# Two stacked fp32 attentions: the score products of the first, K = 16, placed on two 32-row tiles of TensorE

## The reference, cut to what matters

```python
# first block, per image (n = 256 pixels, d = 16)
f, g, hv = xf @ wf + bf, xf @ wg + bg, xf @ wh + bh
beta = softmax(einsum('bnd,bmd->bnm', g, f))
att  = gamma * (einsum('bnm,bmd->bnd', beta, hv) @ wo + bo) + xf
y    = relu(batchnorm(concatenate([att, xf], -1) @ wc + bc))
# second block: 8 heads of 16; keys and values from a 3x3 stride-2 average pool of y
out  = softmax(q @ k.T / 4) @ v          # 256 queries, 64 keys, per head
res  = (out @ w_o + b_o) + y
```

## Time and profile before

| what | us |
|---|---|
| median of 3 runs | 57.96 |
| lowest and highest of the 3 | 57.37, 60.24 |
| span of the profiled execution, first to last instruction | 58.4 |

### The profile page before, as it was taken

One profiled execution on the slowest core, in us unless ns is written; L12 is line 12 of the kernel. 1 busy time (PEld: TensorE's weight loads), 2 busy tenths in 40 slices (PEclk: granted clock), 3 DMA queues, 4 the chain that ended last, 5 costly groups with the idle time before them and its releaser, 6 DMA issues.

```text
span 58.4 us, 948 instructions
## 1 busy us (share of the span) xinstructions
PE 53.0 (91%) x314; PEld 41.1 (70%) x314; DVE 40.1 (69%) x114; ACT 30.5 (52%) x75; POOL 13.5 (23%) x25
## 2 busy tenths in 40 slices
PE   2998999999999999999999999999999999489630
PEld 2935584988786647899966899975889953459410
DVE  1005599300687819996979997998997989997920
ACT  4502333540766997999840899850785810443000
POOL 6779990000019000008300004700004000000000
PEclk9999999999999999999999999999999999999855
DMA  0798200000000000000000000000000200002211
GB/s 0 180 324 334 110 0 0 0 0 0 0 0 0 0 11 0 0 0 6 6 0 0 0 0 0 0 0 11 0 0 0 90 0 0 0 0 83 97 45 45
DMA packets 1300, 1.96 MB, mean 34 GB/s; under 512 B 144, under 2 KB 912, under 8 KB 1296
## 3 DMA queue, kind: packets, MB, share of 16 engines
q1 hardware_dynamic: 1296, 1.91, 9.9%
HBM read 1.38 MB, written 0.52 MB: 33 GB/s over the span
## 4 chain that ended last, share of the span: by engine, by line
PE 84%; DVE 9%; issue 1%; ACT 1%
PE bk_o L391 11%; PE bk_k L350 8%; PE bk_y L323 7%; PE bk_s1a L370 7%; PE bk_fg L266 5%; PE bk_s1b L370 4%; PE bk_s0a L300 4%; PE bk_y L319 4%; PE bk_s0b L300 4%; PE bk_s1b L376 4%; PE bk_k L416 4%; PE bk_fg L338 3%; PE bk_s0a L310 3%; DVE d L638 2%; PE bk_y L357 2%; PE bk_s1a L376 2%
## 5 line engine op out<-in xcount | busy, mean ns | idle before, releaser
L518 ACT ACTIVATE p<-d 128x512 f32<-128x512 f32 x8 | 5.0, 630 | 7.8 <-DVE d L638 7.7
L238 POOL TENSOR_TENSOR p0n<-p,rsum 128x256 f32<-128x256 f32 x6 | 3.5, 612 | 23.5 <-DVE rsum L594 23.5
L391 PE MATMUL bk_o<-v_heads,pt 128*128 128x34 f32 x56 | 6.9, 276 | 0.0
L391 PEld LDWEIGHTS bk_o<-v_heads,pt 128*128 128x128 f32 x56 | 6.6, 192 | 0.1
L350 PE MATMUL bk_k<-xp,late 128*80 128x64 f32 x64 | 5.3, 235 | 0.0
L584 DVE TENSOR_REDUCE nmax<-bk_s0a 128x1 f32<-128x256 f32 x4 | 1.7, 420 | 5.2 <-PE bk_s0a L300 5.2
L513 ACT COPY k_heads<-k_rows 32x128 f32<-32x128 f32 x16 | 4.7, 296 | 0.7
L350 PEld LDWEIGHTS bk_k<-xp,late 128*80 128x80 f32 x64 | 4.9, 151 | 0.3 <-DVE xp L603 0.2
L621 DVE COPY k_heads<-k_rows 32x128 f32<-32x128 f32 x16 | 4.4, 277 | 0.3
L323 PE MATMUL bk_y<-pt,val 128*128 128x256 f32 x16 | 4.6, 415 | 0.0
L370 PE MATMUL bk_s1a<-k_heads,q_heads 128*128 128x512 f32 x8 | 4.3, 615 | 0.1
(11 more groups left out here) (115 smaller groups left out, 113.5 us busy)
## 6 DMA issues: line engine op xcount, KB each, us to landing
late<-in_late SPq DMA_DIRECT2D x1, 522.5 KB, 5.7
x_rest<-in_x_rest SPq DMA_DIRECT2D x1, 384.0 KB, 4.9
out_t<-res SPq DMA_DIRECT2D x3, 128.0 KB, 1.8
prep<-in_prep SPq DMA_DIRECT2D x1, 291.5 KB, 2.8
first<-in_first SPq DMA_DIRECT2D x1, 153.5 KB, 2.4
out_t<-res SPq DMA_DIRECT2D x2, 64.0 KB, 1.6
```

Source lines behind the costliest of these rows:

```text
L238: nc.gpsimd.tensor_tensor(p0n[:, b, t, :], p0[:, b, t, :], rsum0[:, b, t:t + 1].to_broadcast([P, N]), ALU.mult).then_inc(p0_pool, 1)
L391: last = mm(o_ps[b][s][:, k * 2 * VW:(k + 1) * 2 * VW], pt1[:, b, s, k, :], v_heads[:, b, s * 2 + k % 2].rearrange("m h v -> m (h v)"), st ...
L518: sc.activation(p1[:, b, s, :], d1[:, b, s].rearrange("n h m -> n (h m)"), ACT.Exp, scale=1.0 / TEMP).then_inc(exp1_done, 1)
```

## The change

`wfg` becomes 128 columns wide: f, zeros, f, zeros, g, zeros, g, zeros, each copy of 16 columns at a multiple of 32. One product per image now fills all 128 PSUM partitions. The copies to `f` and `g` take 64 partitions each instead of 16, so that both tensors hold the values at partitions 0 to 15 and again at 32 to 47, with zeros (from the zero columns and zero biases) between. The score product of half `t` contracts over the 32 partitions from 32t instead of over 128: half 0 on rows 0 to 31 of TensorE, half 1 on rows 32 to 63. The two halves already wrote to two PSUM banks. The two memsets and the waits on them go. The DMA `first` grows by 80 columns of 128 rows.

```diff
-FIRST = {"wfg": 48, "bf": 1, "bg": 1, "var": 1, "x0": N}
+FIRST = {"wfg": P, "bf": 1, "bg": 1, "var": 1, "x0": N}
...
-            nc.gpsimd.memset(f[:], 0.0).then_inc(fg_clear, 1)
-            nc.gpsimd.memset(g[:], 0.0).then_inc(fg_clear, 1)
...
-                mm(fg_bank[b][0:48, 0:N], f_("wfg"), image(b), start=True, stop=True).then_inc(fg_ps, 1)
+                mm(fg_bank[b][:, 0:N], f_("wfg"), image(b), start=True, stop=True).then_inc(fg_ps, 1)
...
             def scores_0(b, t):
                 if t == 0:
-                    if b == 0:
-                        pe.wait_ge(fg_clear, 2)
...
-                mm(bk_s0[t][:, 0:N], g[:, b, t * P:(t + 1) * P], f[:, b, :], start=True, stop=True).then_inc(s0_ps, 1)
+                mm(bk_s0[t][:, 0:N], g[t * Q:(t + 1) * Q, b, t * P:(t + 1) * P], f[t * Q:(t + 1) * Q, b, :], start=True, stop=True).then_inc(s0_ps, 1)
...
-                sc.activation(f[0:D0, b, :], fg_bank[b][0:D0, 0:N], ACT.Identity, bias=f_("bf", slice(0, D0))).then_inc(f_kept, 1)
+                sc.activation(f[0:T * Q, b, :], fg_bank[b][0:T * Q, 0:N], ACT.Identity,
+                              bias=f_("bf", slice(0, T * Q))).then_inc(f_kept, 1)
...
-                sc.activation(g[0:D0, b, :], fg_bank[b][32:32 + D0, 0:N], ACT.Identity,
-                              bias=f_("bg", slice(32, 32 + D0))).then_inc(g_act, 1)
+                sc.activation(g[0:T * Q, b, :], fg_bank[b][T * Q:P, 0:N], ACT.Identity,
+                              bias=f_("bg", slice(T * Q, P))).then_inc(g_act, 1)
...
-                if b == 0:
-                    dve.wait_ge(fg_clear, 2)
-                v.tensor_scalar(g[0:D0, b, :], bk_fg[32:32 + D0, 0:N], f_("bg", slice(32, 32 + D0)), None,
+                v.tensor_scalar(g[0:T * Q, b, :], bk_fg[T * Q:P, 0:N], f_("bg", slice(T * Q, P)), None,
                                 ALU.add).then_inc(g_dve, 1)
```

More of the change, by code:

```diff
@@ L161, in build @@
         first_in, x_in, prep_in, late_in = sem("first_in"), sem("x_in"), sem("prep_in"), sem("late_in")
-        warm_clear, fg_clear, y_clear, k_clear, v_clear, v_ones = (
-            sem("warm_clear"), sem("fg_clear"), sem("y_clear"), sem("k_clear"), sem("v_clear"), sem("v_ones"))
+        warm_clear, y_clear, k_clear, v_clear, v_ones = (
+            sem("warm_clear"), sem("y_clear"), sem("k_clear"), sem("v_clear"), sem("v_ones"))
         wsum_made, wow_ps, wow_kept, w3_ps, w3_kept, c_kept = (
@@ L474, in keep_f @@
                 act.wait_ge(fg_ps, b + 1)
-                if b == 0:
-                    act.wait_ge(fg_clear, 2)
-                sc.activation(f[0:D0, b, :], fg_bank[b][0:D0, 0:N], ACT.Identity, bias=f_("bf", slice(0, D0))).then_inc(f_kept, 1)
+                sc.activation(f[0:T * Q, b, :], fg_bank[b][0:T * Q, 0:N], ACT.Identity,
+                              bias=f_("bf", slice(0, T * Q))).then_inc(f_kept, 1)
             def keep_g(b):
                 act.wait_ge(fg_ps, b + 1)
-                sc.activation(g[0:D0, b, :], fg_bank[b][32:32 + D0, 0:N], ACT.Identity,
-                              bias=f_("bg", slice(32, 32 + D0))).then_inc(g_act, 1)
+                sc.activation(g[0:T * Q, b, :], fg_bank[b][T * Q:P, 0:N], ACT.Identity,
+                              bias=f_("bg", slice(T * Q, P))).then_inc(g_act, 1)
             def keep_v0(b):
@@ L784 @@
         "first": packed(FIRST, {
-            "wfg": np.concatenate([l0["wf"], none(C, 32 - D0), l0["wg"]], 1), "bf": col(l0["bf"]),
-            "bg": np.concatenate([none(32, 1), col(l0["bg"])]), "var": col(l0["bn_var"]), "x0": x_t[:, :N]}),
+            "wfg": np.concatenate([l0["wf"], none(C, Q - D0)] * T + [l0["wg"], none(C, Q - D0)] * T, 1),
+            "bf": np.tile(np.concatenate([col(l0["bf"]), none(Q - D0, 1)]), (T, 1)),
+            "bg": np.concatenate([none(T * Q, 1), np.tile(np.concatenate([col(l0["bg"]), none(Q - D0, 1)]), (T, 1))]),
+            "var": col(l0["bn_var"]), "x0": x_t[:, :N]}),
         "prep": packed(PREP, {
```

## The result

The changed kernel is slower. Its four runs took 59.42 to 60.24 us, median 59.83; those of the kernel before 57.37 to 60.24, median 59.09. I had forecast 57.6.

A forecast was written before the change was run, and what follows sets the result against it. PE was taken to bound the kernel, busy 53.0 of 58.4 us. Terms of -0.28 (opening), +0.19 (image 1), -0.59 (`project_fg(2)`, `(3)`) and +0.30 (images 2 and 3) gave -0.38: 57.6 us, range 57.2 to 58.0, wider 56.6 to 58.6.

The forecast's parts named there:

- the base: Starting time: profiled span of 58.41 us, taken to lie 0.45 above the median of 57.96 us.
- the price of the opening: Work up to the clock's rise at 14.2 us: -0.38 us at the slow clock, of which -0.28 was taken.
- the clock rises later: Rival, chance 0.08: 32-row products count for less activity or the rise falls worse, warm work runs at half speed; 59.4 us.
- Larger transfer and `project_fg(0)`: Opening: `first` grows by 40 KB, +0.13 us; `project_fg(0)` loads 128 weight columns from idle, +0.09 us.
- Memsets and copies: Removing the two memsets and their waits is worth 0; wider copies of f and g cost 0 more.
- Overlap: Score-product pairs take three records of four: 0.65 us warm (0.86 before), 1.28 cold (1.70); -0.43 us for image 0.
- the full overlap: Rival, chance 0.17: both halves of a score pair run in the time of one; sum -1.01, 56.95 us.
- Changes of shape: On PE, a product of another shape ahead costs the work behind it 0.15 to 0.19 us through an exposed weight load.
- Image 1: Pair's first score product ends 0.19 us later, delaying DVE's `max_0(1,0)` and what queues behind it: +0.19 us.
- Images 2 and 3: Score pair plus shape changes takes 0.99 us against 0.86: +0.13 to 0.17 each, +0.30 us for both.
- `project_fg(2)`, `(3)`: Each falls from 0.56 to 0.43 us and work behind loses 0.19: -0.64, taken as -0.59 us because of DVE's key spread.
- `project_fg(1)`: Opening: its start stays exposed, 1.02 becomes 1.04 us (+0.02); `turn_0(0,0)` behind it falls from 0.62 to 0.43 (-0.19).

The follow-up runs named there:

- e1: The kernel before again, no edit: 57.35 us median (56.95 to 60.18), ratio to itself 1.001; profiled run 57.40 us.
- e7: Kernel before with 128 moving columns instead of 256 in image 0's two score products, warm-up products moved to the other bank half: 59.43 to 59.86 us, ratio 1.044.
- e15, e12: One further profile of the changed kernel, no edit: 59.88 us.
- e8: Changed kernel plus one unused 128 x 128, 256-column product behind image 0's tiled pair: 57.41, 57.42, 59.58 and three at 60.63 to 60.95 us, median 60.10.
- e5: Changed kernel with image 0's score products back on all 128 rows, images 1 to 3 on tiles: 57.09, 59.10 and four at 60.36 to 61.00 us.
- e17: e5 combined with the memset of the keys cut in two as in e10: 57.78 us in one run, 60.44 to 60.57 in five.
- e6: Changed kernel with six warm-up products in place of four: 58.98 to 60.10 us; profiled run 59.11 us.
- e4: Changed kernel with both halves of the score product on rows 0 to 31: 58.81 to 61.27 us, median 59.67; profiled run 61.21 us.
- e2: The changed kernel again, no edit: 59.54 to 59.99 us, ratio 1.045 to the kernel before.
- e11: One further profile of the changed kernel, no edit: 59.75 us.
- e14: One further profile of the changed kernel, no edit: 59.67 us.
- e3: Kernel before with only the projection widened to 128 columns, copies of 64 partitions: three runs at 56.70 to 57.40 us, three at 59.32 to 59.40.
- e10: Kernel before with the keys' memset cut in two, images 1 to 3 behind DVE's two divisions of image 0: 55.56 to 60.22 us, median 56.68, ratio 0.977.

## Why the prediction was wrong

**The step that failed** is the base and, behind it, the price of the opening: "that execution lies 0.45 above the median of 57.96", and "PE had then been without a pause since 4.91", with one rise at 14.2 us taken as the kernel's only way to run. 1.8 us of every time lie outside the span, so the profile was of a 60.2 us run. In e1 the same program has the fast clock from its first score product on and is 2.8 us shorter. The change's sum applies to the run that I had. There its total came near: the change's median of 59.75 stands against 60.25, the median of the 15 long runs of before, -0.50 where I had -0.38. That is partly luck, since the pair was worth twice what I had and the projections less, as the terms below show. The rival at 0.08, "the clock rises later", names the right part of the chip, but its price of 59.4 came out by luck: it took slow work up to 17.89 us, and the change rises at 12 to 14, no later than the 14.2 of the profile before. What is gone is the early rise near 5 us, which I hadn't seen and had in no rival.

**What the runs show of the cause.** The durations of e1 against those of the first profiles show what is lost: the fast clock from 5 to 13 or 14 us, and with it 2.8 us. e7 shows that the shorter pair alone loses the short time, with all rows in use; so no product on 32 rows is needed for it. Whether such products count for less besides isn't tested. e15 against e8 shows one way: a rise near 5 us that is lost at 8 us in the change and kept with one more product. The counts agree for the short time (under 58.3 us): 45 of 65 before, 2 of 6 with the filler, none of 15 in the change, none of 6 in e7.

**What stays open.** Six of seven profiles of the change don't rise early at all, and by the mean clock 14 of its 15 runs don't. What keeps the early rise away there isn't shown. The shorter pair alone doesn't (e7). The wide projection with its larger transfer is the nearest suspect: with it alone 3 of 6 are short, and with it and a full pair 1 of 6 (e5), 1 of 6 (e17). It makes PE begin `project_fg(0)` at 3.2 to 3.3 us, 0.1 later, behind a pause. With six warm-up products, which leave no pause, five of six runs rose early by the mean clock (e6). Six runs each can't separate these shares, and no run has the larger transfer alone.

**The terms of the sum,** at the late rise:

- *Larger transfer and `project_fg(0)`:* PE starts 0.12 us later (3.28 for 3.16; I had 0.13), and takes 1.22 for 1.10 (+0.12 for +0.09). Right.
- *Memsets and copies:* right, nothing. The copy of g takes 0.49 us for 0.47.
- *Overlap:* wrong. I took three records of four; the measured pair is 1.21 us for 2.04 cold, -0.83 for my -0.43, the full overlap that I gave 0.17. The timeline of the change shows why: the records don't come as A1 A2 B1 B2.

```profile
13.76 0.48 PE L296 MATMUL bk_s0a<-f,g 32*128 32x256 f32 x1
13.77 0.48 PE L296 MATMUL bk_s0b<-f,g 32*128 32x256 f32 x1
14.08 0.37 PE L296 MATMUL bk_s0a<-f,g 32*128 32x256 f32 x1
14.09 0.37 PE L296 MATMUL bk_s0b<-f,g 32*128 32x256 f32 x1
```

  The second half's first record starts 0.01 us behind the first half's. The Trainium skill (TensorE: Matmul & The Clock Gate, section The mechanism) has starts in program order. For the two products as wholes this trace agrees, since A starts 0.01 us ahead of B; but the second record of A starts 0.31 us behind the first of B. What failed is what I had drawn from the rule, that both records of A must come ahead of B.
- *Changes of shape:* right. 0.19 us ahead of a pair (0.62 against 0.43 in e4), 0.15 behind it (0.59 against 0.44).
- *Image 1:* right. From `scores_0(1,0)` to `keys_values(0)` it is 15.93 - 13.83 = 2.10 us, and 1.90 before, +0.20 for +0.19.
- *Images 2 and 3:* right in size by luck, for another reason. The pair and `turn_1` together lose 0.64 + 0.59 - 0.86 - 0.44 = -0.07, and then PE waits for `xp`, so that `keys_values` takes 1.35 in place of 1.14. A pass takes +0.13 us: 9.16 (28.92 to 38.08 in the chain) for 9.03, and 9.04 with the projection alone.

```profile
28.92 0.86 PE bk_s1a L366 x2
...
38.08 0.86 PE bk_s1a L366 x2
```

- *`project_fg(2)`, `(3)`:* right mechanism, size off. From `keys_values(0)` to the end of `scores_1(0,0)` -0.42 us (3.67 + 1.02 for 4.06 + 1.05), where I had -0.59. `scores_1(0,0)` comes behind the spread keys, as said, but they are done at 19.29 us and its load begins only at 19.49, with no releaser in the profile; it ends 0.17 later than I allowed.
- *`project_fg(1)`:* 1.15 for 1.02, +0.13 for my +0.02; `turn_0(0,0)` 0.50 for 0.62, and 0.43, as forecast, in four further profiles of the change (e2, e11, e12, e14).

## What to carry to other kernels

Check which of a kernel's times the profile belongs to before taking anything off it: compare the span plus what lies around it with every timed run, and where the times fall into two groups, get a profile of each. In a short kernel the early clock of TensorE can be worth more than all the edits together (3 us here, against 0.5 for the whole change), and shortening the work ahead of a stretch of small products and waits can lose it (e7). Tiling rows pays where a pair of products sets the end; here DVE's `xp` did, and the change of shape on both sides took the rest.

## What the hardware showed that I had not expected

- DVE's division from SBUF to SBUF took 1.00 to 1.99 us while POOL wrote its memsets (e3, e1; the earlier it began, the longer, for it ended at 8.7 to 9.0 us each time), and 0.35 without them (e10). Moved away, that memset is worth 2.3 to 2.5% to the kernel before.
- The clock can fall late, too, with PE at work. The clock line of the page of e4, in 40 slices of 1.5 us, has it at half at about 48 to 50 us, behind `attend_1`, whose products have 34 columns. `scores_1(3,0)` takes 2.03 us there and 1.11 in e1:

```profile
PEclk9999999999999999999999999999999955999985
```

- An unused product may make a kernel faster in some runs: e8's best are 1.8 us under the change's best, though its median is 0.35 over.
